# Attention stage: exponentials kept in SBUF, work by three tiles instead of two, and whole-set operations on VectorE

## The reference

```
K = (x @ Wk + bk).reshape(N, HEADS, DK)
Q = (x @ Wq + bq).reshape(N, HEADS, DK)
V = (x @ Wv + bv).reshape(N, HEADS, DV)
att = jnp.exp(jnp.einsum('ehd,ehd->eh', Q[receivers], K[senders]) / sqrt(DK))
denom = jax.ops.segment_sum(att, receivers, num_segments=N)
att = att / denom[receivers]
msg = att[:, :, None] * V[senders]
agg = jnp.zeros((N, HEADS, DV), dtype=V.dtype).at[receivers].add(msg)
out = jax.nn.relu(agg).reshape(N, HEADS * DV)
out = jax.nn.relu(out @ Wa + ba)
out = jax.nn.relu(out @ Wf + bf)
return x + out
```

## Time and profile before

| | us |
|---|---|
| median of 3 runs | 905.95 |
| lowest and highest | 905.36, 906.53 |
| the profiled execution | 907.27 |
| span of its trace | 905.5 |

### The profile page before, as it was taken

The page is one execution under the profiler, slowest core; times in us unless marked ns, Lnnn a source line. Parts: engine busy times, 40 slices in busy tenths (PEclk is TensorE's granted clock), DMA queues, the critical chain, the costliest instruction groups (busy, mean ns, idle before and its releaser), DMA issues.

```text
span 905.5 us, 11877 instructions
## 1 busy us (share of the span) xinstructions
PE 863.5 (95%) x3978; PEld 492.8 (54%) x3978; DVE 522.0 (58%) x1365; ACT 288.9 (32%) x560; POOL 154.0 (17%) x168
## 2 busy tenths in 40 slices
PE   3999998999998999999999998999999999999898
PEld 2565556745577443344356586546645745654374
DVE  7687777666675899999955484222222223122472
ACT  4531111200104656565434431212222222322273
POOL 6100003200100000000001222234422222222240
PEclk9999998999999999999999998999999999999999
DMA  9410000000418350501022515688989888886722
GB/s 273 158 48 0 1 1 1 1 0 1 167 60 175 76 115 1 114 4 44 11 105 55 179 34 208 252 301 306 318 302 322 312 321 278 325 301 220 182 69 91
DMA packets 41340, 129.81 MB, mean 143 GB/s; under 512 B 8393, under 2 KB 8835, under 8 KB 40639
## 3 DMA queue, kind: packets, MB, share of 16 engines
q1 hardware_dynamic: 32955, 110.76, 37.9%
q0 software_dynamic: 7872, 17.94, 5.4%
q10 hardware_dynamic: 452, 0.34, 0.2%
HBM read 118.48 MB, written 19.68 MB: 153 GB/s over the span
## 4 chain that ended last, share of the span: by engine, by line
PE 67%; DVE 15%; DMA 5%; DVEq 5%; issue 4%; ACT 2%; POOL 1%; SPq 1%; POOLq 0%; ACTq 0%
DVE att L929 8%; PE ps L1464 8%; PE ps L1714 7%; PE ps L1640 7%; PE ps L1732 6%; PE ps L1626 5%; DMA Zg<-z_d,gat 4%; PE ps L1442 4%; PE ps L1498 4%; PE ps L1591 4%; PE ps L1507 4%; PE ps L1425 3%; PE ps L1582 2%; PE ps L1704 2%; PE ps L1783 2%
## 5 line engine op out<-in xcount | busy, mean ns | idle before, releaser
L1073 DVE TENSOR_SCALAR hgT<-ps,cols 128x128 f32<-128x128 f32 x152 | 51.8, 403 | 153.0 <-PE ps L1704 152.9
L929 DVE TENSOR_TENSOR att<-ps,C 125x832 f32<-125x832 f32 (+1 forms) x120 | 119.2, 1005 | 5.6 <-ACT ps L1245 4.9
L1245 ACT ACTIVATE ps<-ps 125x832 f32<-125x832 f32 (+1 forms) x120 | 96.4, 847 | 62.5 <-PE ps L1543 62.5
L1554 PE MATMUL ps<-att,V 125*64 125x416 f32 (+1 forms) x480 | 100.7, 530 | 1.4 <-DVE att L929 1.0
L1626 PE MATMUL ps<-hT,Ws_s 128*128 128x250 f32 x320 | 75.2, 387 | 0.4 <-issue 0.4
L1640 PE MATMUL ps<-Ws_s,hsT 128*125 128x512 f32 x160 | 75.3, 608 | 0.0
L1714 PE MATMUL ps<-W,hgT 128*64 128x256 f32 x576 | 71.6, 392 | 1.0 <-DVE hgT L1073 1.0
L1464 PE MATMUL ps<-mW,xnT 128*125 128x512 f32 x160 | 72.2, 594 | 0.0
L1626 PEld LDWEIGHTS ps<-hT,Ws_s 128*128 128x128 f32 x320 | 60.5, 194 | 20.4 <-issue 13.7
L1732 PE MATMUL ps<-W,ehT 128*64 128x512 f32 x288 | 68.0, 592 | 0.7 <-ACT ehT L1323 0.7
L1543 PE MATMUL ps<-Qst,Kst 128*125 128x416 f32 (+1 forms) x240 | 66.1, 386 | 2.2 <-DVE att L929 1.2
(11 more groups left out here) (249 smaller groups left out, 1208.3 us busy)
## 6 DMA issues: line engine op xcount, KB each, us to landing
W<-in_W SPq DMA_DIRECT2D x144, 512.0 KB, 6.3
Kst<-qk_d SPq DMA_DIRECT2D x32, 156.2 KB, 5.4
Qst<-qk_d SPq DMA_DIRECT2D x32, 156.2 KB, 5.6
Yt<-y_d SPq DMA_DIRECT2D x10, 448.0 KB
Ws_s<-in_Ws SPq DMA_DIRECT2D x2, 2048.0 KB, 9.7
qk_d<-qk_hi POOLq DMA_DIRECT2D x4, 625.0 KB, 3.4
qk_d<-qk_lo POOLq DMA_DIRECT2D x4, 625.0 KB, 4.6
z_d<-yz POOLq DMA_DIRECT2D x10, 250.0 KB, 2.7
```

Source lines behind the costliest of these rows:

```text
L929: V_.tensor_tensor(att[:, n % 3, :, 0:w], scores_of(n, w), C[:, s, o:o + w].unsqueeze(1).to_broadcast([P, 2, w]), ALU.mult).then_inc(att_m ...
L1073: i = V_.tensor_scalar(hgT[:, u, k, :], bank(u, 128, 128, k * 128), col("g1", k), col("b1ln", k), ALU.mult, ALU.add)
L1245: S_.activation(b, b, ACT.Exp, scale=float(DK) ** -0.5).then_inc(s_exp, 1)
L1554: k = MM(sums_of(i, 64 * j, 64, w), V[:, s, pair, j:j + 2, :], att[:, n % 3, j, 0:w], start=s == 0, stop=s == T - 1, skip_group_check=True)
```

## The change

The exponential is written into a new ring `es` of four places in SBUF instead of over the scores in PSUM, and VectorE multiplies from there. `att` becomes a ring of five. `scores(n)` then waits for `s_exp` of tile n-3 instead of `att_made`, the exponential of tile n waits for `att_made` of tile n-4, and the multiplication of tile n waits for `att_used` of tile n-5. TensorE works in groups of three: the scores of three tiles, then the sums of the three before. `keep_heads` has five steps instead of nine: one transpose of 416 (or 448) columns, the addition and reciprocal, one transpose back, and one multiplication for each head. They are placed after the multiplications of s = 4 to 8.

```diff
+EB, AB, GP = 4, 5, 3
-        att = ph("att", [P, 3, 2, 420], F32, 116)
+        att = ph("att", [P, AB, 2, 420], F32, 134)
+        es = ph("es", [P, EB, 2, 420], F32, 150.5)
...
-                if step < 2:
-                    if step == 0:
-                        v.wait_ge(att_used, T * i + T)
-                    c = slice(224 * step, (224, w32)[step])
-                    V_.transpose(sumsT[:, c], sums_of(i, 0, 128, w32)[:, c])
+                nb = w32 // 32
+                if step == 0:
+                    v.wait_ge(att_used, T * i + T)
+                    V_.transpose(sumsT[:, 0:w32], sums_of(i, 0, 128, w32))
+                elif step == 1:
...
-                    h = 2 * pair + j
-                    c = slice(208 * half, (208, w)[half])
-                    k = V_.scalar_tensor_tensor(aggT[32 * (h % 4):32 * (h % 4) + 32, h // 4, o + c.start:o + c.stop],
-                                                sums_of(i, 96 * j, 32, w)[:, c], 0.0, rden[32 * j + 32:32 * j + 64, c], ALU.max, ALU.mult)
-                    if step == 8:
+                    k = V_.scalar_tensor_tensor(aggT[32 * (h % 4):32 * (h % 4) + 32, h // 4, o:o + w],
+                                                sums_of(i, 96 * j, 32, w), 0.0, rden[32 * j + 32:32 * j + 64, 0:w], ALU.max, ALU.mult)
+                    if j:
                         k.then_inc(head_kept, 1)
...
-                if n >= 3:
-                    v.wait_ge(att_used, n - 2)
...
-                if i >= 1 and s >= 1:
-                    keep_heads(i - 1, s - 1)
-            for step in range(9):
+                if n >= AB:
+                    v.wait_ge(att_used, n - AB + 1)
+                V_.tensor_tensor(att[:, n % AB, :, 0:w], es[:, n % EB, :, 0:w], C[:, s, o:o + w].unsqueeze(1).to_broadcast([P, 2, w]), ALU.mult).then_inc(att_made, 1)
+                if i >= 1 and 4 <= s < 9:
+                    keep_heads(i - 1, s - 4)
+            for step in range(5):
...
-                b = scores_of(n, w)
-                S_.activation(b, b, ACT.Exp, scale=float(DK) ** -0.5).then_inc(s_exp, 1)
+                if n >= EB:
+                    a.wait_ge(att_made, n - EB + 1)
+                S_.activation(es[:, n % EB, :, 0:w], scores_of(n, w), ACT.Exp, scale=float(DK) ** -0.5).then_inc(s_exp, 1)
...
-                    pe.wait_ge(att_made, n - 2)
+                    pe.wait_ge(s_exp, n - 2)
...
-            scores(0)
-            scores(1)
-            for n in range(0, SETS * T, 2):
-                for k in (n + 2, n + 3):
-                    if k < SETS * T:
-                        scores(k)
-                sums(n)
-                sums(n + 1)
+            for n in range(GP):
+                scores(n)
+            for first in range(0, SETS * T, GP):
+                for n in range(first + GP, min(first + 2 * GP, SETS * T)):
+                    scores(n)
+                for n in range(first, first + GP):
+                    sums(n)
```

More of the change, by code:

```diff
@@ L896, in keep_heads @@
                 w32 = w + -w % 32
-                if step < 2:
-                    if step == 0:
-                        v.wait_ge(att_used, T * i + T)
-                    c = slice(224 * step, (224, w32)[step])
-                    V_.transpose(sumsT[:, c], sums_of(i, 0, 128, w32)[:, c])
+                nb = w32 // 32
[3 more added lines that the diff above has]
+                elif step == 1:
+                    v.drain()
+                    V_.tensor_scalar(dens[:, 0:nb], sumsT[:, 0:w32:32], TINY, None, ALU.add)
+                    v.drain()
+                    V_.reciprocal(dens[:, 0:nb], dens[:, 0:nb])
@@ L902, in keep_heads @@
                 elif step == 2:
                     v.drain()
-                    V_.tensor_scalar(dens[:, 0:w32 // 32], sumsT[:, 0:w32:32], TINY, None, ALU.add)
-                    v.drain()
-                    V_.reciprocal(dens[:, 0:w32 // 32], dens[:, 0:w32 // 32])
-                elif step < 5:
+                    V_.transpose(rden[:, 0:w32].rearrange("p (b q) -> p b q", q=32),
+                                 dens[:, 0:nb].unsqueeze(2).to_broadcast([128, nb, 32]))
+                else:
@@ L908, in keep_heads @@
                     if step == 3:
                         v.drain()
-                    c = slice(7 * (step - 3), (7, w32 // 32)[step - 3])
-                    V_.transpose(rden[:, 32 * c.start:32 * c.stop].rearrange("p (b q) -> p b q", q=32),
-                                 dens[:, c].unsqueeze(2).to_broadcast([128, c.stop - c.start, 32]))
-                else:
-                    if step == 5:
-                        v.drain()
-                    j, half = divmod(step - 5, 2)
+                    j = step - 3
```

3 lines of the change are left out of this document (1 added, 2 removed).

## The result

The changed kernel takes 899.57 us (median of 7 runs, 893.22 to 901.14), the kernel before 905.95 (904.48 to 908.81, 7 runs). The ratio is 0.9921, with a 95% interval of 0.9894 to 0.9949: between 4.6 and 9.6 us less. The profiled execution took 901.14 us (span 899.2) against 907.27 (span 905.5). Forecast were 896.4 with a range of 889.0 to 901.5. The time lies in the range, but above the forecast's own range of 894.5 to 898.5.

What follows compares the result with a forecast made beforehand. VectorE was taken to bound from the second set: 13.35 - 0.18 - 0.58 = 12.59 us a set. The stage ends at 441.0 instead of 450.6, so 905.95 - 9.6 = 896.4 us; own range 894.5 to 898.5, with rivals 889 to 901.5.

Steps and rivals of the forecast that it cites:

- What sets the pace: Attention stage: TensorE paces the first set, VectorE the later ones, only 0.85 us a set apart.
- The saving of the whole-width steps: VectorE's work on the sums: transposes save 0.18 us a set, the multiplications for the heads 0.58.
- The SBUF source: VectorE's multiplication by C reading SBUF instead of PSUM: no change taken, 0.07 us a tile less kept as a bound.
- The stage's start: First sets: tile 14's multiplication starts at 305.2 us and the first transpose at 306.15.
- rival 2: Rings do not cover the uneven rhythm: VectorE idles some 0.4 us a set, 4 us back, 900.4 us; chance 0.20.
- TensorE's group: TensorE's scores and sums: 3.58 us for three tiles, 1.19 a tile, 11.93 a set against 12.50.
- ScalarE: Exponentials written to SBUF: 852 ns for 832 columns, about 10 more than now, under 0.9 us a tile; nothing to pay.
- Rival 1: VectorE reads SBUF quicker, 0.07 us a tile less: 11.9 us a set, 6.6 more gained, 889.8 us; chance 0.12.
- The tightest place: Group of s = 8, 9 and 0: tile s = 4 readable at 4.37, VectorE there at 4.70, 0.3 us to spare.
- Rival 3: Gain given back behind the stage: one more experts' gather uncovered, 6.5 us, 902.9 us; chance 0.05.
- Rival 4: VectorE's multiplication with two SBUF operands collides with GpSimd: about 0.45 us a tile, 50 us, 946 us; chance 0.04.
- Rival 5: No gain within the measurement, VectorE's pace set by something else such as the gaps: 905 to 906 us; chance 0.04.

Runs made afterwards that it cites:

- experiment 5: Kernel before with only the five whole-width steps, spread behind s = 1, 3, 5, 7 and 9: 896.20 us, ratio 0.9899, 12.65 us a set.
- experiment 1: Changed kernel with TensorE in groups of two instead of three, rings and whole steps kept: 913.28 us, 14.07 us a set.
- experiment 3: Kernel before with only five whole-width steps behind s = 4 to 8, exponentials in PSUM, groups of two: 913.8 us, 13.94 us a set.
- experiment 6: Changed kernel with groups of two and the steps spread behind s = 1, 3, 5, 7 and 9: 898.33 us, 12.77 us a set.
- experiment 4: Changed kernel with both SBUF rings at three places instead of four and five: 904.03 us, 13.16 us a set.
- experiment 7: Changed kernel with the multiplication by C of tile s = 6 moved to GpSimd: 906.16 us, 13.54 us a set.
- experiment 2: Changed kernel with the old nine half-width steps behind s = 1 to 9, rings and groups of three kept: 906.21 us, 13.48 us a set.
- experiment 8: Kernel before with five whole steps behind s = 4 to 8 and groups of three, exponentials in PSUM: 960.56 us, 18.28 us a set.

## Why the prediction was right or wrong

**What sets the pace** was right: VectorE from the second set on, TensorE in the first. After the change VectorE has no idle time ahead of a multiplication from 307.7 us on.

**The saving of the whole-width steps** was right in mechanism and size. The prediction had 0.76 a set (0.18 and 0.58); experiment 5, which has nothing else, measured 13.38 - 12.65 = 0.73; it needs the steps spread, or the rings and groups, to arrive (experiments 1 and 3). The step from a whole transpose to the tile behind it takes 0.54 (421.83 to 422.37; worked out 0.53). A head costs 0.72 over a tile (426.53 to 428.19 is 1.66, less 0.94; worked out 0.73).

**The SBUF source** was taken at no change, from the duration in the earlier trace rows. The duration was right, but a set pays 0.12 at the first transpose (experiments 5 and 6; where it comes from stands at the end of this section). This is the term that failed: the prediction priced the added operand by its own instruction and not by the step to the one behind it, and it said that a whole-width operation dearer than its halves, or a step that moves by over 0.03, would spoil it. With 0.03 from the base (13.38, not 13.35) and 0.03 from the saving, it makes 12.59 into 12.77, 0.18 a set, **1.8 us over ten sets**.

**The stage's start.** The first transpose came at 306.89, not 306.15. The first exponential was 0.22 later. Some 0.1 came with the first sums. The rest, 0.4, was an error of working: tile 14's multiplication was let start at 305.2, when its exponential was ready, but VectorE has tiles 12 and 13 to do first (304.08 + 2 x 0.94 = 305.96). Together 0.74. The two misses sum to 2.5, and the first matmul of Wa indeed came at 443.57 instead of 441.0. The measured 899.57 lies nearer to the 900.4 of rival 2 than to the forecast of 896.4, so the number alone would have pointed to a cause that the trace does not show: VectorE never waits for the rings.

**TensorE's group** was right to the hundredth, 3.58. But its 11.93 a set is not what bounds this kernel, so groups of three by their rate shorten only the first set. What they do in the rest, together with the rings, is to cover the bunching: 13.94 in experiment 3, 14.07 with the rings alone, 13.16 with groups and rings of three, 12.77 with all.

**ScalarE** was right: 867 ns each, and it waits for TensorE 54 us in all. The Trainium skill, in "ScalarE: Activation LUTs", section "Step-by-step: what each stage is for", has it that PSUM is written faster than SBUF; the trace agrees in sign, by 20 ns (847 to 867), twice what the prediction took from the copies, and all of it is hidden.

**Rival 1** (SBUF read quicker) is out: 1010 ns against 1005. The estimate of 0.065 us less from the Trainium skill, "VectorE: DVE Perf Modes", section "The TRN2 errata", is not borne out here. **Rival 2** (rings do not cover) did not occur, and experiment 4 shows how near it was: with less depth VectorE idles 0.46 us in two sets of three, which take 0.50 longer, at the last tiles ahead of the bunch. The tightest place by the prediction, the tile s = 4, with 0.3 us to spare, held, and it is in the trace: in one set of three the exponential of that tile ends 0.27 us before its multiplication starts (395.01 and 395.29), and in another the same holds one tile earlier. **Rival 3** (given back behind) was not what happened as described: 0.7 us more behind the stage, less than the scatter of this part, at the same mean clock. **Rival 4** (collision) is a matter of GpSimd at work (experiment 7); in this kernel it rests there. The row taken for it was the mean of 811 and 1508 ns, so the estimate of 0.45 a tile was too low for a tile that is caught. **Rival 5** (no gain) is out: the interval leaves 4.6 to 9.6 us, and the sets are 0.61 shorter.

**The late transpose.** Why does the first transpose of a set start 0.03 behind the multiplication and not 0.08 or 0.09 ahead of its end when the multiplications read SBUF? It does not wait for the sums: those it needs ended 3.2 us or more before it in the changed kernel from the second transpose on. The rings' depth and the group's size are not it either (experiments 4, 1 and 6). The source alone is not the answer: in the changed kernel the transpose of the first set (306.89) still starts 0.09 ahead of the end of the multiplications (304.08 + 2.90 = 306.98). What separates the two kinds in every trace is **where VectorE last read PSUM**. The transpose reads PSUM from partition 0 on. Ahead of each of the 70 late ones (ten in each of the seven kernels with exponentials in SBUF and transposes) VectorE's last read of PSUM was the second head's multiplication, which begins at partition 96 (`sums_of(i, 96 * j, 32, w)` with j = 1); the multiplications in between read SBUF only. Ahead of the early ones it was a read from partition 0: the multiplication itself where the exponentials lie in PSUM, the first half transpose for the second half of experiment 2, and earlier work in the first set, where no head has been multiplied yet. No transpose but those that wait for their sums departs from this. It is a pattern of the traces, and no run tried it by itself: one small read of PSUM from partition 0 behind the second head, or the heads in the other order, would tell.

## What to carry to other kernels

Fewer, wider operations on the limiting engine do bring what their rows say, but where they stand decides whether it arrives: cost the worst run of neighbours, not the set's mean, and try spreading them evenly before buying buffers to cover the bunch (12.65 us a set without new buffers, 12.77 with them, 13.94 bunched and uncovered). The same holds for an engine that has time over: the same four small operations cost 0.5 us a set where they push a group's exponentials back and nearly nothing in the gap where that engine waits anyway (12.45 and 11.97 us a set, against TensorE's 11.93). And an instruction's price is the step to the next one, which can hang on what stood well ahead of it. When a working lets an instruction start as soon as its input is ready, check the queue ahead of it on its own engine.

## What the runs showed of the hardware

- A float32 multiplication of 125 x 832 on VectorE that starts behind one of GpSimd's (1.96 us) ends 0.88 or 0.89 us after GpSimd's end and so takes up to 2.77 us, against 0.98 alone. A small addition of 128 x 14 caught in the same way takes 1.75 us (experiment 7).
- Behind multiplications that read SBUF, the first transpose from PSUM of each later set starts 0.11 to 0.12 us later than behind ones that read PSUM; its second half, where it is split, does not. In all 70 cases VectorE's last read of PSUM ahead of it began at partition 96; ahead of the early ones it began at partition 0.
- TensorE was at the lower clock level (0.50, 1.2 GHz) from 288.8 to 295.4 us in both runs in which it had stood 1.59 and 1.79 us for the DMA of `Qst`, until 286.75 and 287.02 (experiments 3 and 5). The same kernel as in experiment 5, without that wait in its timed rounds' profile, kept 1.00 from 290 to 294 us, and so did the kernel after. It is not the only way there: in experiment 8, with 0.23 us of that wait, the mean from 290 to 294 us was 0.61.
- Between two groups of scores and sums TensorE spends a fixed part: 2.50 us for two tiles, 3.58 for three, so 1.08 for a tile and 0.34 for the change there and back.
- On ScalarE a logarithm from PSUM of 32 x 416 takes 602 ns and an exponential from SBUF of that size 550, against 867 for one of 125 x 832: half the columns and a quarter of the partitions still cost two thirds.
